# A graph layer on one core: key sums that begin with the rows left in SBUF, weights loaded between key blocks, rows split one at a time, edge lists loaded further apart

## The chip, the cores and the metric

The kernel runs on one core of a Trainium2 chip. TensorE (PE) multiplies matrices into PSUM; VectorE (DVE), ScalarE (ACT) and GpSimd (POOL) work on SBUF (POOL not on PSUM); SyncE (SP) here only issues DMAs. Each engine works through its own queue in order and waits on semaphores. The metric is the time of one execution in microseconds (us), lower is better; the runs of the kernel before lie within 0.12 us of each other.

## What is computed

One layer of a graph network with attention and a mixture of experts, on 12,500 nodes of 256 features with 200,000 edges of 8 types, sorted by destination:

```python
xn = _layernorm(x, axis=-1)
x = x + _L0_gnn_ref(xn, ...) + _L0_mix_ref(xn[None], ...)[0]
x = x + _L0_ffn_ref(_layernorm(x, axis=-1)[None], ...)[0]
```

The graph part multiplies each edge's source row by its weight, averages over the edges with the same type and destination, multiplies by that type's matrix and adds `x @ root + bias`. The mix part is linear attention: `q` and `k` go through `elu + 1`, `kv` and `k_sum` are sums over all nodes of `k` times `v` and of `k`, and each node's output is `q @ kv / (q @ k_sum)` through `wo`. The last part is a router over six experts of three layers, of which the best two are combined.

## The kernel before

Rows are worked on in *tiles* of 128 nodes (`NT`; 98 of them, `TILES_N`) and *row blocks* of four tiles (`SUB`; 25, `SUPER`, the last with two tiles). Products are made exact by splitting each factor into a high and a low part, three matmuls for one.

**First stage** (about 16 to 618 us). Per tile `u`, TensorE multiplies the normalised rows by all eight type matrices: four PSUM results of 512 columns, 24 matmuls, in three banks `yb` in turn (L769). ScalarE copies them into `yst` (L350; two buffers, `u % 2`), and SP stores `yst` to `y_tab` in HBM (L283). The copy into a buffer waits for the store of the tile two before (`y_out`). Per row block, SP also stores the transposed rows, high and low (`xhl`, two buffers), to `xt_tab`, stores `xs` to `x_tab` and loads the next `xs`. SP issues everything from one list, in which `edge_loads(u)` stands ahead of tile `u`'s store: four edge lists (`dst`, `etype`, `src`, `ew`; 125 rows of 1600 numbers each) at tiles 0 to 3, a copy of `dst` to `dpad` at tiles 5 and 6, padding of `etab` at tile 8. VectorE works on the lists in `edges(u)`, between the steps of the row blocks: at tile 5 it waits for all four lists (L641, then L642), from tile 5 on it uses `dst`, from tile 6 on `etype` and `src`, from tile 75 on `ew`. A barrier ends the stage.

**Key stage** (about 623 to 880 us). Twelve *portions* `p`; in the first nine (`KEYED`) the 98 tiles' keys and values are made, 11 tiles to a portion, 10 in the last (`keys_of`). Per tile `v`:

- TensorE: `key_product(v)`, six matmuls of the rows in `xk` with `wk` and `wv` (L1647), into one of three banks; then `key_sum_of(v - 2)`, four matmuls that add the tile into the sum (L1810);
- VectorE: `key_value(v)` adds the bias into `zv` (L1556), then `key_features(v - 1)` finishes `kf_c` (L1561);
- ScalarE: `key_parts(v)`, `ek_c` and `kf_c` (L1251, L1252).

`xk` has two halves of one row block each; SP loads block `d` from `xt_tab` (`load_xk`, L1080) when the products of block `d - 2` are done. Before its loads SP issues the edge tables `tab`, `wq` and `g_root` (into `xn_c`, whose split by ScalarE and VectorE comes ahead of VectorE's first `key_value`), and `xc`; then, between blocks 1 and 2, the first two experts' layers (`load_w`, into `stage`) and the router's. The third layer follows block 10.

Beside the keys, the first row block's edges are gathered (POOL, L1135, from `y_tab` into `ring`) and summed by TensorE, one portion of five or six edge tiles after each portion of keys (`aggregate(0, p - 1)`). Portions below 4 (`PLAIN`) are multiplied unsplit (L1704); from 4 on, ScalarE makes `row_hi` (`high`, L1192), VectorE `row_lo` (`low_rows`, L1379), and TensorE multiplies both (L1710). In key portions 5 to 8, ScalarE does the rows of portion `p - 1` in one go after the third tile, VectorE after the fifth. After portions 2, 5 and 9 (`WEIGHTS_AT`) ScalarE and VectorE split one layer of expert weights. `root(-1, FIRST)`, 24 matmuls, stands after portion 0.

**Last stage** (to the end): per row block, the attention's output, the experts, and the gathers and sums of the next row block.

SBUF names that share memory are allocated one over the other (`with ExitStack() as px`): `xk` lies over the third layer's high part, `zv` over later buffers.

Of the kernel before, what the change touches and what calls it, by code (L numbers as in the profile page):

```python
# [5 lines left out]
F32 = mybir.dt.float32  # L6
# [8 lines left out]
P = 128  # L15
KC = C // P
# [39 lines left out]
def gps_layer(nc, x, src, dst, etype, ew, g_w, g_root, g_b, wq, bq, wk, bk, wv, bv, wo, bo,  # L56
# [21 lines left out]
    with whole:  # L78
# [25 lines left out]
        eq = sbuf(whole, "eq", [P, KC, NS])  # L104

        pa = ExitStack()
        with pa:
# [12 lines left out]
            xhl = sbuf(pa, "xhl", [P, 2, 2, KC, NS], F32R)  # L120
# [66 lines left out]
            wkv_in, wr_in, small_in, bkv_in, rows_in_e, lin_in = (  # L187
                sem(n) for n in ("wkv_in", "wr_in", "small_in", "bkv_in", "rows_in_e", "lin_in"))
# [25 lines left out]
            def _(sp):  # L214
# [208 lines left out]
            def _(dve):  # L423
# [197 lines left out]
                def edges(u):  # L621
# [18 lines left out]
                    if u == 5:  # L640
                        dve.wait_ge(lin_in, 64)  # L641
# [3 lines left out]
                    if u == 6:  # L645
                        dve.tensor_copy(lin_tf, lin_t[0:ROWS, :])
# [188 lines left out]
        with pc:  # L835
# [53 lines left out]
            row_lo = sbuf(pc, "row_lo", [P, SLOTS, PT, C], F32R)  # L889
            xlo = sbuf(pc, "xlo", [P, C], F32R)  # L890
            with ExitStack() as px:
# [12 lines left out]
            xsel = sbuf(pc, "xsel", [P, NT], F32R)  # L904
# [123 lines left out]

            def keys_of(p):
# [17 lines left out]
            def _(sp):  # L1047
# [36 lines left out]
                load_xk(0)  # L1084
# [4 lines left out]
                load_xk(1)  # L1089
                load_table(1)  # L1090
                load_w(0, e_w1, 0)
# [791 lines left out]
```

## Time and profile before

| what | value |
|---|---|
| median of 3 runs | 3027.47 us (3027.4 to 3027.52) |
| the profiled execution's own time | 3028.82 us |
| its span, first to last instruction | 3027.3 us |
| mean granted TensorE clock | 0.988 of full speed |
| busy: PE, DVE, ACT, POOL | 97%, 72%, 58%, 55% |

A row of busy time gives the stretch and its length, then busy us and count of PE, of PE's weight loads (PEld), DVE, ACT and POOL, then three numbers: granted clock, busy share of the 16 DMA engines, GB/s moved. A row in order of time gives start, length, engine, line, operation, out<-in and, in brackets, the idle time before it with what ended it. SPq is SP's queue. A DMA row ends with KB each and us from issue to landing, where that is known.

### The profile page before, as it was taken

How to read it: one execution, taken by the hardware profiler on the slowest of the kernel's cores; microseconds unless marked ns; L12 is line 12 of the kernel's file. 1: busy time of each engine (PE TensorE's matmuls, PEld its weight loads, DVE VectorE, ACT ScalarE, POOL GpSimd, SP SyncE). 2: the span in 40 equal slices, each digit the busy share in tenths (PEclk: the TensorE clock that was granted, in tenths of full speed). 3: DMA queues.
4: the chain of work that ended last, by engine and by line, in shares of the span. 5: the costliest groups of instructions: out<-in, count | busy, mean ns of one | idle time of the engine just before them, and what ended most of it. 6: DMA issues, size and time to landing. Idle time of an engine off the chain costs nothing.

```text
span 3027.3 us, 47261 instructions
## 1 busy us (share of the span) xinstructions
PE 2934.1 (97%) x16707; PEld 2567.4 (85%) x16708; DVE 2189.2 (72%) x5317; ACT 1765.7 (58%) x3392; POOL 1659.3 (55%) x1700
## 2 busy tenths in 40 slices
PE   6999999969989999999999999999999999999998
PEld 5888878858778888888888888888888888888887
DVE  4479664125668787778888777788777778878775
ACT  3555555523446665666666566666666566666555
POOL 1000000042257777777777777777777777777740
PEclk9999999989999999999999999999999999999999
DMA  7677677875443444444444444443444444344420
GB/s 258 249 267 272 261 276 269 292 250 174 146 140 107 129 131 132 133 127 129 118 121 133 133 134 129 131 122 118 134 131 131 134 126 129 116 128 131 131 74 11
DMA packets 182224, 473.45 MB, mean 156 GB/s; under 512 B 46934, under 2 KB 105260, under 8 KB 159747
## 3 DMA queue, kind: packets, MB, share of 16 engines
q0 software_dynamic: 80544, 221.54, 25.4%
q1 hardware_dynamic: 99248, 247.02, 22.6%
q8 instruction: 133, 2.18, 0.3%
q10 hardware_dynamic: 2196, 1.86, 0.2%
q14 instruction: 103, 0.84, 0.1%
HBM read 312.80 MB, written 158.29 MB: 156 GB/s over the span
## 4 chain that ended last, share of the span: by engine, by line
PE 68%; DVE 6%; ACT 2%; DVEq 1%; issue 1%; DMA 1%; SPq 0%; ACTq 0%
PE bank L1647 45%; PE acc L1704 8%; PE acc L1710 8%; PE acc L1647 2%; DVE sel L1362 2%; PE bank L1674 1%; PE bank L1810 1%; DVE x L1457 1%; PE bank L1683 1%; PE bank L1693 1%; DVE stats_c L1461 1%; PE bank L1760 1%; DVEq L1459 1%; DVE h_lo L1487 1%; ACT h_hi L1205 1%
## 5 line engine op out<-in xcount | busy, mean ns | idle before, releaser
L1135 POOL DMA_INDIRECT ring<-y_tab,tab x1666 | 1642.6, 986 | 653.4 <-issue 497.5
L1205 ACT ACTIVATE h_hi<-bank,bias_t 128x512 fp32r<-128x512 f32 (+1 forms) x600 | 407.7, 679 | 315.6 <-PE bank L1647 280.1
L1487 DVE TENSOR_TENSOR h_lo<-bank,h_hi 128x512 fp32r<-128x512 f32 (+1 forms) x600 | 382.1, 675 | 228.1 <-ACT bank L1206 226.2
L769 PE MATMUL yb<-wr_hi,xhl 128*128 128x512 f32 x1568 | 509.4, 402 | 14.5 <-ACT yst L350 12.5
L1192 ACT ACTIVATE row_hi<-ring,tab 128x256 fp32r<-128x256 f32 x1091 | 449.6, 497 | 14.4 <-PE acc L1710 13.5
L1379 DVE SCALAR_TENSOR_TENSOR row_lo<-ring,tab,row_hi 128x256 fp32r<-128x256 f32 x1091 | 447.8, 478 | 7.8 <-ACT row_hi L1192 7.8
L350 ACT ACTIVATE yst<-yb 128x512 f32<-128x512 f32 x392 | 229.8, 596 | 273.6 <-PE yb L769 245.5
L1206 ACT ACTIVATE bank<-bank,bias_t 128x512 f32<-128x512 f32 (+1 forms) x600 | 386.3, 644 | 0.0
L769 PEld LDWEIGHTS yb<-wr_hi,xhl 128*128 128x128 f32 x1568 | 298.6, 190 | 88.8 <-ACT yst L350 15.2
L1647 PE MATMUL bank<-ew_hi,h_hi 128*128 128x256 f32 x1176 | 342.7, 291 | 1.5 <-DVE h_lo L1487 1.4
L1647 PE MATMUL bank<-ew_lo,h_hi 128*128 128x256 f32 x1176 | 329.1, 280 | 0.0
L1647 PE MATMUL bank<-ew_hi,h_lo 128*128 128x256 f32 x1176 | 328.9, 280 | 0.0
L769 PE MATMUL yb<-wr_lo,xhl 128*128 128x512 f32 x784 | 312.9, 399 | 0.0
L1710 PE MATMUL acc<-row_hi,hot_r 128*128 128x256 f32 x1091 | 270.5, 286 | 8.5 <-DVE row_lo L1379 8.5
L1710 PE MATMUL acc<-row_lo,hot_r 128*128 128x256 f32 x1091 | 268.0, 284 | 0.0
L1704 PE MATMUL acc<-ring,sel 128*128 128x256 f32 x1150 | 264.5, 379 | 0.0
L1647 PE MATMUL bank<-h_hi,ew_hi 128*128 128x512 f32 (+1 forms) x600 | 237.0, 395 | 2.0 <-DVE h_lo L1487 2.0
L1704 PEld LDWEIGHTS acc<-ring,sel 128*128 128x128 f32 x1150 | 214.4, 190 | 28.3
L1529 DVE SCALAR_TENSOR_TENSOR y<-bank,gate,y 128x256 f32<-128x256 f32 x490 | 211.6, 477 | 36.9 <-PE bank L1647 30.9
L1647 PE MATMUL bank<-h_hi,ew_lo 128*128 128x512 f32 (+1 forms) x600 | 234.2, 390 | 0.0
L1647 PE MATMUL bank<-h_lo,ew_hi 128*128 128x512 f32 (+1 forms) x600 | 234.2, 390 | 0.0
L1647 PE MATMUL bank<-ft_hi,ew_hi 128*128 128x512 f32 (+1 forms) x600 | 233.0, 388 | 0.0
(265 smaller groups left out, 5514.7 us busy)
## 6 DMA issues: line engine op xcount, KB each, us to landing
y_tab<-yst SPq DMA_DIRECT2D x97, 1024.0 KB, 4.1
ring<-y_tab,tab POOLq DMA_INDIRECT x1666, 2.8
xt_tab<-xhl SPq DMA_DIRECT2D x25, 1024.0 KB, 4.6
xk<-xt_tab SPq DMA_DIRECT2D x25, 1024.0 KB, 4.9
xc<-xt_tab SPq DMA_DIRECT2D x25, 1024.0 KB, 5.4
x<-x_tab SPq DMA_DIRECT2D x49, 256.0 KB, 3.2
xs<-in_x SPq DMA_DIRECT2D x24, 512.0 KB, 6.0
x_tab<-xs SPq DMA_DIRECT2D x24, 512.0 KB, 5.0
```

Of the source, the lines that this page charges most:

```text
L350: act.activation(yst[:, h, 2 * b:2 * b + 2, :], yb[(YB * u + b) % 3][:, :].rearrange("p (r n) -> p r n", r=2), ACT.Copy).then_inc(y_ev, 1)
L769: last = pe.matmul(out_ap, a, b, start=(i == 0), stop=(i == len(parts) - 1))
L1135: pool.indirect_dma_start(out=out_ap, out_offset=None, in_=y_tab[:, :], in_offset=bass.IndirectOffsetOnAxis(ap=idx_ap, axis=0)).then_inc(s ...
L1192: last = act.activation(row_hi[:, p % BUFS, q, :], ring[:, p % SLOTS, q, :], ACT.Copy, scale=tab[:, n % 2, t, k, 2:3])
L1205: act.activation(dest[:, m, 0:W], b[:, 0:W], ACT.Relu, bias=bias)
L1206: act.activation(b[:, 0:W], b[:, 0:W], ACT.Relu, bias=bias).then_inc(h_set, 1)
L1379: last = dve.scalar_tensor_tensor(out=row_lo[:, p % SLOTS, q, :], in0=ring[:, p % SLOTS, q, :], scalar=tab[:, n % 2, t, k, 2:3], in1=row_h ...
L1487: gone(dve.tensor_tensor(lo_[:, m, 0:W], bank[plan[kind, (e, m)][0]][:, 0:W], hi[:, m, 0:W].bitcast(F32), ALU.subtract))
L1529: last = dve.scalar_tensor_tensor(out=y[:, t, :], in0=b[:, (t % 2) * C:(t % 2 + 1) * C], scalar=gate[:, t, e:e + 1], in1=(y if e else x1)[ ...
L1647: last = pe.matmul(out_ap, a, b, start=(begin and i == 0), stop=(not more and i == len(parts) - 1), skip_group_check=more)
L1704: last = pe.matmul(sums(t), sel[:, p % BUFS, q, :], ring[:, p % SLOTS, q, :], start=False, stop=False, skip_group_check=True)
L1710: last = pe.matmul(sums(t), hot_r[:, p % BUFS, q, :], half, start=False, stop=False, skip_group_check=True)
```

## The change

The two `xhl` buffers, which hold the last two row blocks (23 and 24) at the end of the first stage, now live on into the key stage and are its `xk`; the key sums begin with these six tiles (`key_order`), and only blocks 0 to 22 are loaded, each when the half it goes into is done. The first layer's weights and the router's load after block 2, the second layer's after block 6. `high` and `low_rows` take a range of rows: counting a portion's tiles from 0, ScalarE does two rows after each of tiles 1 to 3, VectorE one after each tile from 5 on and the rest after the last. The edge lists load at tiles 0, 2, 4 and 8, each with a semaphore of its own, `dpad` at 11 and 12. `qf` and the third layer's high part move so that `xhl` can lie over them; `ek_c` has two buffers instead of three and lies elsewhere.

```diff
         eq = sbuf(whole, "eq", [P, KC, NS])
+        with ExitStack() as px:
+            xhl = sbuf(px, "xhl", [P, 2, 2, KC, NS], F32R)
+        w3_hi = sbuf(whole, "ew2_hi", [P, EXPERTS, KC, C], F32R)
+        qf = sbuf(whole, "qf", [P, KC, NS])
...
-            xhl = sbuf(pa, "xhl", [P, 2, 2, KC, NS], F32R)
...
                 def edge_loads(u):
-                    if u < 4:
-                        a, into = ((dst, lin_d), (etype, lin_t), (src, lin_s), (ew, lin_w))[u]
-                        sp.dma_start(into[0:ROWS, :], by_row(a)).then_inc(lin_in, 16)
+                    if u in (0, 2, 4, 8):
+                        i = (0, 2, 4, 8).index(u)
+                        a, into = ((dst, lin_d), (etype, lin_t), (src, lin_s), (ew, lin_w))[i]
+                        sp.dma_start(into[0:ROWS, :], by_row(a)).then_inc(lin_in[i], 16)
                     whole_tiles = E // P
-                    if u == 5:
+                    if u == 11:
                         sp.dma_start(dpad[0:whole_tiles, :].rearrange("(a t) k -> a (t k)", a=22),
                                      dst[0:whole_tiles * P].rearrange("(a k) -> a k", a=22)).then_inc(dpad_out, 16)
-                    if u == 6:
+                    if u == 12:
...
                     if u == 5:
-                        dve.wait_ge(lin_in, 64)
+                        dve.wait_ge(lin_in[0], 16)
...
                     if u == 6:
+                        dve.wait_ge(lin_in[1], 16)
+                        dve.wait_ge(lin_in[2], 16)
...
+                    if u == 75:
+                        dve.wait_ge(lin_in[3], 16)
...
-                ek = sbuf(px, "ek_c", [P, KEY_BUFS, C])
...
-            qf = sbuf(pc, "qf", [P, KC, NS])
...
-            with ExitStack() as px:
-                xk = sbuf(px, "xk", [P, 2, 2, KC, NS], F32R)
-            w_hi.append(sbuf(pc, "ew2_hi", [P, EXPERTS, KC, C], F32R))
+            w_hi.append(w3_hi)
+            xk = xhl
...
+            with ExitStack() as px:
+                ek = sbuf(px, "ek_c", [P, 2, C])
...
+            KEPT = SUPER - 2
+            key_order = list(range(SUB * KEPT, TILES_N)) + list(range(SUB * KEPT))
+
+            def key_place(d):
+
+                return d % 2 if d >= KEPT else (d + SUPER) % 2
...
                 def load_xk(d):
-                    if d >= 2:
-                        sp.wait_ge(key_proj, SUB * (d - 1))
-                    sp.dma_start(xk[:, d % 2, :, :, :].bitcast(F32).rearrange("p h k n -> p (h k n)"),
+                    sp.wait_ge(key_proj, SUB if d == 0 else SUB * d + LAST_T)
+                    sp.dma_start(xk[:, key_place(d), :, :, :].bitcast(F32).rearrange("p h k n -> p (h k n)"),
                                  xt_tab[d:d + 1, :, :].rearrange("a p n -> (a p) n")).then_inc(xk_in[d % 2], 16)
 
                 sp.sem_inc(y_stored, 16)
-                load_xk(0)
                 load_table(0)
                 for i, w in enumerate((wq, g_root)):
                     sp.dma_start(stage_q[:, i, :, :], w.rearrange("(k p) n -> p k n", p=P)).then_inc(wqr_in, 16)
                 load_xc(0)
-                load_xk(1)
                 load_table(1)
-                load_w(0, e_w1, 0)
-                sp.dma_start(stage_r[:, :, :], r_w1.rearrange("(k p) n -> p k n", p=P)).then_inc(w_in[0], 16)
-                load_w(1, e_w2, 1)
-                for d in range(2, SUPER):
+                for d in range(KEPT):
                     load_xk(d)
+                    if d == 2:
+                        load_w(0, e_w1, 0)
+                        sp.dma_start(stage_r[:, :, :], r_w1.rearrange("(k p) n -> p k n", p=P)).then_inc(w_in[0], 16)
+                    if d == 6:
...
 
-                def high(n, p):
+                def high(n, p, some=range(PT)):
                     if p >= parts(n):
                         return
-                    act.wait_ge(tab_in[n % 2], 16 * SUB * (n // 2 + 1))
-                    act.wait_ge(rows_in[p % SLOTS], 16 * gathers(n, p))
-                    tables_free(act, n, p)
-                    for q, (t, k) in enumerate(tiles_of_portion(p)):
+                    size = len(tiles_of_portion(p))
+                    if some[0] == 0:
+                        act.wait_ge(tab_in[n % 2], 16 * SUB * (n // 2 + 1))
+                        act.wait_ge(rows_in[p % SLOTS], 16 * gathers(n, p))
+                        tables_free(act, n, p)
+                    for q in range(some[0], min(some[-1] + 1, size)):
+                        t, k = tiles_of_portion(p)[q]
                         last = act.activation(row_hi[:, p % BUFS, q, :], ring[:, p % SLOTS, q, :],
                                               ACT.Copy, scale=tab[:, n % 2, t, k, 2:3])
-                    last.then_inc(hi_ready, 1)
+                    if some[-1] >= size - 1:
...
                     if p < KEYED:
                         for j, v in enumerate(keys_of(p)):
                             key_parts(v)
-                            if p > PLAIN and j == 2:
-                                high(0, p - 1)
+                            if p > PLAIN and 1 <= j <= PT // 2:
+                                high(0, p - 1, range(2 * j - 2, 2 * j))
...
 
-                def low_rows(n, p):
+                def low_rows(n, p, some=range(PT)):
                     if p >= parts(n):
                         return
-                    dve.wait_ge(hi_ready, split_before(n, p) + 1)
-                    for q, (t, k) in enumerate(tiles_of_portion(p)):
+                    size = len(tiles_of_portion(p))
+                    if some[0] == 0:
+                        dve.wait_ge(hi_ready, split_before(n, p) + 1)
+                    for q in range(some[0], min(some[-1] + 1, size)):
+                        t, k = tiles_of_portion(p)[q]
                         last = dve.scalar_tensor_tensor(out=row_lo[:, p % SLOTS, q, :], in0=ring[:, p % SLOTS, q, :],
                                                         scalar=tab[:, n % 2, t, k, 2:3],
                                                         in1=row_hi[:, p % BUFS, q, :].bitcast(F32),
                                                         op0=ALU.mult, op1=ALU.subtract)
-                    last.then_inc(lo_ready, 1)
+                    if some[0] < size <= some[-1] + 1:
+                        last.then_inc(lo_ready, 1)
...
-                            if p > PLAIN and j == 4:
-                                low_rows(0, p - 1)
+                            if p > PLAIN and j >= 5:
+                                low_rows(0, p - 1, range(j - 5, j - 4) if j < len(keys_of(p)) - 1 else range(j - 5, PT))
...
                 def key_product(v):
                     if v >= KEY_BUFS:
                         pe.wait_ge(key_z, v - KEY_BUFS + 1)
-                    d, nodes = v // SUB, slice(v % SUB * NT, (v % SUB + 1) * NT)
-                    in_parts(bank[KEY_BANKS[v % KEY_BUFS]][:, :], lambda k: xk[:, d % 2, 0, k, nodes], lambda k: xk[:, d % 2, 1, k, nodes],
+                    u = key_order[v]
+                    d, nodes = key_place(u // SUB), slice(u % SUB * NT, (u % SUB + 1) * NT)
+                    in_parts(bank[KEY_BANKS[v % KEY_BUFS]][:, :], lambda k: xk[:, d, 0, k, nodes], lambda k: xk[:, d, 1, k, nodes],
                              lambda k: wkv_hi[:, k, :], lambda k: wkv_lo[:, k, :]).then_inc(key_proj, 1)
...
-                    n = NT if v < TILES_N - 1 else LAST_ROWS
+                    n = NT if key_order[v] < TILES_N - 1 else LAST_ROWS
...
                     for v in keys_of(p):
-                        if v % SUB == 0:
-                            pe.wait_ge(xk_in[v // SUB % 2], 16 * (v // SUB // 2 + 1))
+                        u = key_order[v]
+                        if u % SUB == 0 and u < SUB * KEPT:
+                            pe.wait_ge(xk_in[u // SUB % 2], 16 * (u // SUB // 2 + 1))
```

## Rows read from the trace of the kernel before

**Rows 1.** Busy time by stretch (start:end, length, then each engine's busy us):
```profile
16.00:76.00 60.00, 49.39 (x185) 38.31 (x186) 26.82 (x44) 24.16 (x44) 3.25 (x12) 0.89 0.71 259
...
76.00:618.00 542.00, 539.73 (x2433) 436.35 (x2431) 306.06 (x490) 282.36 (x519) 7.58 (x6) 1.00 0.72 269
...
618.00:720.00 102.00, 78.40 (x386) 65.93 (x386) 42.61 (x90) 29.93 (x72) 41.29 (x44) 0.87 0.64 216
...
730.00:740.00 10.00, 10.00 (x57) 8.62 (x57) 5.93 (x12) 3.72 (x11) 0.00 (x0) 1.00 0.82 292
...
668.00:670.00 2.00, 2.00 (x19) 2.00 (x18) 0.33 (x1) 0.72 (x2) 1.39 (x3) 1.00 0.35 98
```

**Rows 2.** Waits from 0 to 130 us (total, times, longest):
```profile
ACT yst L350 <- DMA y_tab<-yst: 18.3, 3, 6.7
```

**Rows 3.** DMA issues in narrow windows (count, KB each, us to landing):
```profile
y_tab<-yst SPq DMA_DIRECT2D x1, 1024.0 KB, 17.0
...
lin_w<-in_edge_weight SPq DMA_DIRECT2D x1, 781.2 KB
```

**Rows 4.** Busy time in stretches of 2 us, columns as in Rows 1:
```profile
54.00:56.00 2.00, 1.36 (x3) 1.16 (x4) 0.34 (x2) 1.74 (x4) 0.00 (x0) 0.55 0.32 133
...
56.00:58.00 2.00, 2.00 (x7) 1.54 (x6) 0.00 (x0) 0.40 (x1) 0.00 (x0) 0.60 0.31 131
```

**Rows 5.** SP's queue in order of time, first 130 us:
```profile
36.88 0.62 SPq L283 DMA_DIRECT2D y_tab<-yst  x1
...
76.05 0.33 SPq L283 DMA_DIRECT2D y_tab<-yst  x1
...
99.33 0.32 SPq L283 DMA_DIRECT2D y_tab<-yst  x1
```

**Rows 6.** SP's queue in order of time, 620 to 690 us:
```profile
623.34 0.33 SPq L1080 DMA_DIRECT2D xk<-xt_tab  x1
625.09 3.71 SPq L1073 DMA_DIRECT2D tab<-etab  x4
...
630.35 0.43 SPq L1080 DMA_DIRECT2D xk<-xt_tab  x1
...
635.62 3.06 SPq L1065 DMA_DIRECT2D stage<-in_L_ffn_expert_w  x2
...
644.66 42.52 SPq L1080 DMA_DIRECT2D xk<-xt_tab  x5
```

**Rows 7.** TensorE in order of time, 636 to 662 us (in brackets: idle before):
```profile
639.93 0.71 PE L1810 MATMUL bank<-zv,kf_c 128*128 128x129 f32 x4 [3.39 <-DVE kf_c L1561]
...
659.18 0.79 PE L1647 MATMUL bank<-wkv_hi,xk 128*128 128x512 f32 x1 [7.76 <-DMA xk<-xt_tab]
```

**Rows 8.** Chain that ended last, 590 to 910 us:
```profile
642.56 0.86 PE bank L1810 x4
...
667.71 2.87 PE acc L1647 x24
...
683.17 0.45 PE bank L1810 x4
683.61 1.39 PE bank L1647 x6
```

**Rows 9.** Loads of xk alone, issues at 671.99 and 630.35:
```profile
xk<-xt_tab SPq DMA_DIRECT2D x1, 1024.0 KB, 5.1
...
xk<-xt_tab SPq DMA_DIRECT2D x1, 1024.0 KB, 10.9
```

**Rows 10.** Waits from 720 to 884 us:
```profile
PE bank L1810 <- DVE kf_c L1561: 10.5, 8, 3.4
```

**Rows 11.** VectorE and ScalarE in order of time, 769 to 782 us:
```profile
775.34 0.69 DVE L1556 TENSOR_TENSOR zv<-bank,kw_sb 128x512 f32<-128x512 f32 x1 [0.81 <-PE bank L1647]
...
776.51 2.46 DVE L1379 SCALAR_TENSOR_TENSOR row_lo<-ring,tab,row_hi 128x256 fp32r<-128x256 f32 x6
...
773.03 2.49 ACT L1192 ACTIVATE row_hi<-ring,tab 128x256 fp32r<-128x256 f32 x6
```

More of the change, by code:

```diff
@@ L186, in gps_layer @@
             wkv_hi_set, wkv_split = (sem(n) for n in ("wkv_hi_set", "wkv_split"))
-            wkv_in, wr_in, small_in, bkv_in, rows_in_e, lin_in = (
-                sem(n) for n in ("wkv_in", "wr_in", "small_in", "bkv_in", "rows_in_e", "lin_in"))
+            wkv_in, wr_in, small_in, bkv_in, rows_in_e = (
+                sem(n) for n in ("wkv_in", "wr_in", "small_in", "bkv_in", "rows_in_e"))
+            lin_in = [sem(f"lin_in{i}") for i in range(4)]
             pads_set, ident_set, consts_set, misc_full, misc_free = (
@@ L889, in gps_layer @@
             row_lo = sbuf(pc, "row_lo", [P, SLOTS, PT, C], F32R)
+            with ExitStack() as px:
+                ek = sbuf(px, "ek_c", [P, 2, C])
             xlo = sbuf(pc, "xlo", [P, C], F32R)
+            xsel = sbuf(pc, "xsel", [P, NT], F32R)
+            spare = sbuf(pc, "spare", [P, NT])
             with ExitStack() as px:
@@ L903, in gps_layer @@
             xtab_i = xtab[:, :].bitcast(I32)
-            xsel = sbuf(pc, "xsel", [P, NT], F32R)
             xrel = sbuf(pc, "xrel", [P, 1])
@@ L1088, in _ @@
                 load_xc(0)
-                load_xk(1)
                 load_table(1)
-                load_w(0, e_w1, 0)
-                sp.dma_start(stage_r[:, :, :], r_w1.rearrange("(k p) n -> p k n", p=P)).then_inc(w_in[0], 16)
-                load_w(1, e_w2, 1)
-                for d in range(2, SUPER):
+                for d in range(KEPT):
                     load_xk(d)
+                    if d == 2:
+                        load_w(0, e_w1, 0)
+                        sp.dma_start(stage_r[:, :, :], r_w1.rearrange("(k p) n -> p k n", p=P)).then_inc(w_in[0], 16)
+                    if d == 6:
+                        load_w(1, e_w2, 1)
                     if d == 10:
@@ L1183, in queries @@
                         act.activation(b[:, 0:NS], b[:, 0:NS], ACT.Relu, bias=bias_t[:, BQ + m:BQ + m + 1]).then_inc(q_set, 1)
-                def high(n, p):
+                def high(n, p, some=range(PT)):
                     if p >= parts(n):
                         return
-                    act.wait_ge(tab_in[n % 2], 16 * SUB * (n // 2 + 1))
-                    act.wait_ge(rows_in[p % SLOTS], 16 * gathers(n, p))
-                    tables_free(act, n, p)
-                    for q, (t, k) in enumerate(tiles_of_portion(p)):
+                    size = len(tiles_of_portion(p))
[5 more added lines that the diff above has]
+                        t, k = tiles_of_portion(p)[q]
                         last = act.activation(row_hi[:, p % BUFS, q, :], ring[:, p % SLOTS, q, :],
                                               ACT.Copy, scale=tab[:, n % 2, t, k, 2:3])
-                    last.then_inc(hi_ready, 1)
+                    if some[-1] >= size - 1:
+                        last.then_inc(hi_ready, 1)
                 def iteration(i, plan):
@@ L1250, in key_parts @@
                     z = zv[:, v % KEY_BUFS, 0:KC, 0:P]
-                    act.activation(ek[:, v % KEY_BUFS, :].rearrange("p (k n) -> p k n", k=KC), z, ACT.Exp)
+                    act.activation(ek[:, v % 2, :].rearrange("p (k n) -> p k n", k=KC), z, ACT.Exp)
                     act.activation(kf[:, v % 2, :].rearrange("p (k n) -> p k n", k=KC), z, ACT.Relu).then_inc(key_e, 1)
@@ L1560, in key_features @@
                     dve.wait_ge(key_e, v + 1)
-                    dve.scalar_tensor_tensor(out=kf[:, v % 2, :], in0=ek[:, v % KEY_BUFS, :], scalar=1.0, in1=kf[:, v % 2, :],
+                    dve.scalar_tensor_tensor(out=kf[:, v % 2, :], in0=ek[:, v % 2, :], scalar=1.0, in1=kf[:, v % 2, :],
                                              op0=ALU.min, op1=ALU.add).then_inc(key_f, 1)
```

## Prediction

> **What bounds the kernel now.** I read the busy time by stretch first: it says where TensorE, the engine of the whole kernel, is not busy. In the first stage (76 to 618 us) it is busy 539.7 of 542 us; what is lost lies in 16 to 76 us (10.6 us idle, granted clock 0.89) and in 618 to 720 us (23.6 us idle, clock 0.87) [rows 1]. The change touches both stretches, and the rest of the key stage besides. So each stretch needs its own question: which wait ends last there.
>
> In 16 to 76 us the waits say it: ScalarE, which copies PSUM to `yst`, waited three times, 18.3 us, for an earlier `y_tab` store out of the same buffer [rows 2]. Store 2 took 17.0 us to land [rows 3]. While ScalarE waits, only 0.32 and 0.31 of the 16 DMA engines work, at 133 and 131 GB/s [rows 4]: that is 5 of 16 (0.3125). The stage's other DMAs have 128 partitions, the edge lists 125 rows; so I read it as five engines carrying the lists, with every store's last five shares queued behind them. SP's queue gives the price: stores 2 to 6 lie 39.17 us apart, stores 6 to 10, with no list left, 23.28 [rows 5]. The lists cost 15.9 us.
>
> In 618 to 720 us TensorE has three holes: it starts only with its first `xk`, asked for at 623.34 [rows 6], waits 3.39 us for VectorE (639.93), and 7.76 us for its third `xk` (659.18) [rows 7]. SP's queue shows why the third is late: four weight loads of 768 KB and the router's 128 KB were issued from 635.62 on, and `xk` block 2 only at 644.66 [rows 6].
>
> **Part 1, edge lists spaced.** Bytes and instructions stay the same. One of five engines moves 132/5 = 26.4 GB/s [rows 4]; a list of 781.2 KB [rows 3] then holds the five for 6.0 us, a 1 MB transfer split over 16 holds each for 2.5, a half MB for 1.25. Four tiles (23.3 us) carry four stores, a transposed row block and two half MB, 15.0 us per engine; 8.3 us are spare, or 2.1 per tile. A list needs three tiles of spare time and gets two, then two, then four: the queue still grows, but half as much.
>
> I walk the five engines' queue. First before, as a test: free at an estimated 29.8 after list 0, then store 0, half MB, list 1, store 1, half MB, list 2, store 2: 29.8 + 3 x 2.5 + 2 x 1.25 + 2 x 6.0 = 51.8; it landed at 36.88 + 17.0 = 53.9 [rows 3, 5]. The walk is 2 us early, so I add 2. After the change one list fewer lies ahead of store 2: 47.8, 10.9 us after its issue. Then the transposed block and store 3 (5.0), the next list (6.0) and store 4 (2.5): 61.3, 11.2 us after an issue at about 50.1 (36.88 + 2 x 5.82 + 1.6). How late may a store be? The next tile (5.8) and three PSUM banks (3 x 1.4) pass before TensorE halts, less 0.7 for the copy: 9.3. The halts are 1.6 and 1.9, together 3.5; the fourth list, four tiles later, meets a drained queue. After a halt of 3 us the clock granted was 0.55 and 0.60 over 4 us [rows 4], which loses 1.7; I count 2.0 for both halts. Gain: 15.9 - 5.5 = 10.4. Bounds: no halt at all, 15.9; both stores 2.5 us later than walked, 5.
>
> `dpad` (781 KB, DRAM to DRAM) moves from tile 5 to 11; its reader waits in tile 27, some 90 us on, so I cost it at nothing; without that cover it would be one halt of 3 us. The list waits of VectorE are split; the second stands at tile 6 behind list 2 (walked to 58.8), and behind it queue VectorE's split of the next row block, which TensorE needs two tiles later, about 10 us: hidden. The wait for `lin_w` in tile 75 costs nothing: the list has then been in for some 350 us.
>
> **Part 2, key sums start with rows in SBUF.** Removed: two of 25 `xk` loads, and the wait of the first product. TensorE may start some 5 us earlier, but its fourth product waits for VectorE's `zv`, which comes behind its work on `wq` and `g_root`. Those loads move up by the removed issue, at most 625.09 - 623.34 = 1.75 us, at least 0 [rows 6]; I take 1.0. So the first key sum starts at 638.9, not 639.93 [rows 7]; product 3, which ended at 642.56 [rows 8], ends at 641.5. That asks for block 0 into the freed half. A load issued alone while gathers still ran took 5.1 us [rows 9]: it lands at 646.6. Two more tiles (1.84 each: 0.45 + 1.39 [rows 8]) and about 1.5 of half clock end at 646.7, so it just fits. Products 6 to 10 take 5 x 1.84, and `root` starts at 656.0 instead of 667.71 [rows 8]: 11.7. I take 11.5, for a little wait.
>
> The weights then follow block 2. It is asked for when product 9 ends, at about 653.6; behind it in the queue stand 1.70 MB of weights and, from 663.8, block 3. From 641.25 (630.35 + 10.9) to 659.15 SP's queue moved 4.33 MB beside the gathers [rows 6, 9]: 242 GB/s. Block 2, weights and block 3 are 3.80 MB, 15.7 us and some 1.5 to land: 670.8. Product 18 needs block 3 at 656.0 + 2.87 + 7 x 1.84 = 671.7. It fits by 0.9 us. The second weights follow block 6, when the gathers have slowed; the third load shows such a meeting (730 to 740 us, DMA at 0.82, TensorE busy 10.0 of 10 [rows 1]). Bounds for the part: block 0 late by 3 us with a half-clock stretch behind it, and block 3 late by 1.5: 6; a prologue 1.75 earlier: 12.5.
>
> A rule speaks against this. The gathers run in the other queue, at 98 GB/s when alone [rows 1]. The Trainium skill, "DMA: Bandwidth & Descriptors", section "Queues, rings and completion order", says that each DMA engine goes round the queues that have work, a packet from each. By that, the gathers could take half of each engine, block 0 would land some 2.5 us later, and the part would give 9 instead of 11.5. The 5.1 us of the load at 672, gathers beside it, do not bear this out; it is case (f) below.
>
> **Part 3, rows one by one.** The same 23 splits. The eight waits of TensorE for `kf_c` in 720 to 884 us sum to 10.5 [rows 10]; two, 2.9 and 3.4, are the weight splits and stay, about 4.1 are the six-row bursts of 2.46 (VectorE) and 2.49 us (ScalarE) [rows 11] and the stage's end. In pieces they fit: a row costs VectorE 0.41, and it sits idle 0.81 per tile [rows 11]; two rows cost ScalarE 0.83 beside its 0.72 per tile of 1.84. That gains 3.3. Against it: in portions 5 and 7 the last row comes after the portion's last tile, and the aggregate waits for it: `zv` 0.65, `kf_c` 0.42 and the row 0.41 end 1.5 after the last product, where 0.3 was the case: 1.2. In portion 5 the weight split's wait swallows it; portion 7 pays it. At the end two rows come ahead of the last `kf_c`: 0.4. Net 1.5; bounds -1 and 3.3. The smaller `ek` costs nothing: a third copy was never in use, for key sum v-2 must be done before `ek` v is written.
>
> **Sum.** 10.4 + 11.5 + 1.5 = 23.4. The profiled execution took 3028.82 around a span of 3027.3; the median of the runs is 3027.47, 1.35 less. I take the sum from the median: 3004.1 us.
>
> **Rivals.** (a) The halts of the first stage persist, since the lists still ride on five engines: gain 5 there, 18 in all, 3009.5. For it: the walk missed by 2 us, and both late stores lie under 2 us past the limit. (b) Loads late in the key start, block 0 and then block 3 behind the weights: 6 instead of 11.5, 3009.6. The margin of block 0 is 0.1 us, that of block 3 is 0.9. (c) Nothing moves, because the losses reappear as other waits (VectorE's prologue in the key stage, five engines in the first): 3027. Against it: TensorE is idle or at half clock there, and behind these stretches it is busy all the time. (d) Slower: each `xk` load is asked for only when its half is free, four tiles or 7.34 us ahead. If the mean landing, 5.1 here, rose past 7.34 + 23.4/23 = 8.36 us in all 23 loads, the gain would be gone; at 9.5 us, 3030. Against it: the lead is the same as in the kernel before, where loads behind no weights cause no wait. (e) Better: no halts and no late row, under 2997. (f) The gathers take half of each engine while both queues have work: 16 x 26.4 = 422 GB/s [rows 4] halved makes 5.0 us of a load's 2.5, so block 0 lands at 649.1 and the part gives 9: 3006.6. For it: block 0 does fall among the gathers; against it: at 98 GB/s they use a quarter of 422.
>
> **Chances.** Forecast 0.62 (own range 2999 to 3009), (a) 0.15, (b) 0.08, (c) 0.04, (d) 0.02, (e) 0.04, (f) 0.05. From 2996 to 3014 leaves out (c), (d), part of (e), and (a) where (b) joins it. Under 3021.4 is faster by over 0.2%, about what a measurement here can tell: 0.94; within 0.2% 0.04; slower 0.02.
>
> **What would show it.** Right: stores 2 to 6 about 29 us apart; two short halts in the first 80 us; no wait for `xk` over 1 us after the key stage's start; `root` near 656; no 1 us holes in portions 5 to 8 but a wait for `row_lo` before portion 7's aggregate. Wrong: halts of 3 us as before, a product at 647 or 671 that waits for its load, or a new wait for `kf_c` in each tile that carries rows.

## The result, and the profile after

The changed kernel takes 2992.3 us (median of 4 runs, 2990.83 to 2996.88) against 3027.43 (4 runs) beside it: a ratio of 0.989, 95% interval 0.9876 to 0.9904. The gain is 35.1 us where 23.4 were predicted, and the time lies under the range. The profiled execution is the slowest of the four (2996.88 us, span 2995.4), so its parts sum to 31.9 us.

The kernel after, busy time by stretch, columns as in [rows 1]:

```profile
16.00:76.00 60.00, 53.95 (x226) 43.16 (x227) 33.33 (x59) 28.93 (x53) 3.31 (x12) 0.97 0.74 281
76.00:600.00 524.00, 518.69 (x2390) 427.98 (x2388) 299.38 (x476) 276.90 (x508) 7.60 (x6) 1.00 0.74 276
600.00:720.00 120.00, 101.94 (x512) 86.20 (x512) 58.93 (x124) 38.70 (x96) 49.76 (x50) 0.90 0.65 213
```

The first and third rows are what the prediction was about. The second is the surprise. TensorE was busy 539.7 of 542 us there before [rows 1] and is busy 518.7 of 524 now: hardly less full, yet the stage ends sooner than store 6 explains. SP's queue of the kernel after, in order of time (it answers to [rows 5]), and the last store before:

```profile
36.81 0.33 SPq L288 DMA_DIRECT2D y_tab<-yst  x1
...
65.35 0.32 SPq L288 DMA_DIRECT2D y_tab<-yst  x1
...
89.98 0.32 SPq L288 DMA_DIRECT2D y_tab<-yst  x1
...
600.80 0.33 SPq L288 DMA_DIRECT2D y_tab<-yst  x1
```
```profile
618.54 0.33 SPq L283 DMA_DIRECT2D y_tab<-yst  x1
```

Stores 2 to 6 lie 28.54 us apart, and store 6 goes out 10.7 us earlier, as forecast. But the last store is 17.7 us earlier: between store 10, 9.35 us earlier, and the last another 8.4 came in, over 87 tiles. TensorE in order of time in a stretch of 2 us without a halt, first before, then after:

```profile
399.72 0.63 PE L769 MATMUL yb<-wr_hi,xhl 128*128 128x512 f32 x2
400.18 0.39 PE L769 MATMUL yb<-wr_lo,xhl 128*128 128x512 f32 x1
400.42 0.63 PE L769 MATMUL yb<-wr_hi,xhl 128*128 128x512 f32 x2
...
401.12 0.63 PE L769 MATMUL yb<-wr_hi,xhl 128*128 128x512 f32 x2
```

```profile
399.87 0.61 PE L778 MATMUL yb<-wr_hi,xhl 128*128 128x512 f32 x2
400.32 0.39 PE L778 MATMUL yb<-wr_lo,xhl 128*128 128x512 f32 x1
400.55 0.61 PE L778 MATMUL yb<-wr_hi,xhl 128*128 128x512 f32 x2
...
401.23 0.61 PE L778 MATMUL yb<-wr_hi,xhl 128*128 128x512 f32 x2
```

Three products take 0.70 us before and 0.68 after: a start every 233 and every 227 ns, of the same instructions, at a granted clock of 1.00 in both. Busy time can't show that, since a slower product is as busy as a quick one.

The key stage of the kernel after, TensorE in order of time (it answers to [rows 7]; in brackets the idle time before), two pieces of the chain ([rows 8]; start, length, what), and last TensorE in the kernel before:

```profile
599.75 0.39 PE L778 MATMUL yb<-wr_hi,xhl 128*128 128x512 f32 x1
607.35 0.79 PE L1670 MATMUL bank<-wkv_hi,xhl 128*128 128x512 f32 x1 [7.21 <-DVEq L1329]
...
621.69 1.23 PE L1834 MATMUL bank<-zv,kf_c 128*128 128x129 f32 x4 [7.18 <-DVE kf_c L1584]
...
631.13 0.50 PE L1670 MATMUL bank<-wkv_hi,xhl 128*128 128x512 f32 x1 [0.75 <-DMA xhl<-xt_tab]
...
695.60 0.80 PE L1834 MATMUL bank<-zv,kf_c 128*128 128x129 f32 x2 [2.92 <-DVE kf_c L1584]
...
848.27 0.58 PE L1733 MATMUL acc<-row_hi,hot_r 128*128 128x256 f32 x1 [6.41 <-DVE row_lo L1401]
```

```profile
625.51 5.57 DMA xhl<-xt_tab
...
640.55 2.87 PE acc L1670 x24
```

```profile
617.48 0.40 PE L769 MATMUL yb<-wr_hi,xhl 128*128 128x512 f32 x1
630.15 0.77 PE L1647 MATMUL bank<-wkv_hi,xk 128*128 128x512 f32 x1 [12.27 <-DMA xk<-xt_tab]
...
722.63 0.71 PE L1810 MATMUL bank<-zv,kf_c 128*128 128x129 f32 x4 [2.92 <-DVE kf_c L1561]
...
882.75 0.58 PE L1710 MATMUL acc<-row_hi,hot_r 128*128 128x256 f32 x1 [6.41 <-DVE row_lo L1379]
```

TensorE starts earlier after the first stage (7.21 us instead of 12.27), waits more for the first key sum (7.18 instead of 3.39), and reaches `root` some 40 us after the stage's end instead of 50. No load of `xk` is waited for longer than 0.75 us.

For all runs I read three lengths from such rows. S is the issue of the last `y_tab` store. K runs from the end of the stage's last product to the product behind the 2.9 us wait (here 600.14 to 695.60: 95.46). R runs from there to aggregate(0, 9) (to 848.27: 152.67). Behind that the program does the same work: an undisturbed iteration takes 87.60 us in both. S, K and R are each read from one profiled execution.

### The profile page after: what moved, and what is told of

Same layout as the page of the kernel before. It is cut to its first block, busy times and chain, and to the rows that moved or that the text cites. A ratio compares the mean times of both kernels' runs of the same rounds, so it can differ in the third digit from the quotient of the medians.

```text
span 2995.4 us, 47258 instructions
## 1 busy us (share of the span) xinstructions
PE 2914.0 (97%) x16707; PEld 2561.0 (85%) x16708; DVE 2190.0 (73%) x5317; ACT 1762.9 (59%) x3392; POOL 1674.2 (56%) x1700
## 4 chain that ended last, share of the span: by engine, by line
PE 63%; POOL 6%; DVE 5%; issue 3%; ACT 1%; DVEq 1%; DMA 0%; SPq 0%; ACTq 0%; POOLq 0%
PE bank L1670 41%; PE acc L1727 7%; PE acc L1733 7%; POOL ring L1150 6%; PE acc L1670 2%; DVE sel L1381 2%; PE bank L1834 1%; PE bank L1697 1%; DVE x L1480 1%; PE bank L1706 1%; PE bank L1716 1%; DVE h_lo L1510 1%; DVE stats_c L1484 1%; PE bank L1783 1%; DVEq L1482 1%
## 5 line engine op out<-in xcount | busy, mean ns | idle before, releaser
L778 PE MATMUL yb<-wr_hi,xhl 128*128 128x512 f32 x1568 | 498.2, 394 | 13.1 <-ACT yst L355 11.1
L1210 ACT ACTIVATE row_hi<-ring,tab 128x256 fp32r<-128x256 f32 x1091 | 451.7, 498 | 33.3 <-issue 17.7
L778 PE MATMUL yb<-wr_lo,xhl 128*128 128x512 f32 x784 | 306.9, 391 | 0.0
L1733 PE MATMUL acc<-row_hi,hot_r 128*128 128x256 f32 x1091 | 270.1, 286 | 10.7 <-DVE row_lo L1401 10.7
```

What stands on the lines that cost most here:

```text
L778: last = pe.matmul(out_ap, a, b, start=(i == 0), stop=(i == len(parts) - 1))
L1210: last = act.activation(row_hi[:, p % BUFS, q, :], ring[:, p % SLOTS, q, :], ACT.Copy, scale=tab[:, n % 2, t, k, 2:3])
L1733: last = pe.matmul(sums(t), hot_r[:, p % BUFS, q, :], half, start=False, stop=False, skip_group_check=True)
```

## The experiments

| kernel | median, us | ratio to before (95%) | S | K | R |
|---|---|---|---|---|---|
| before | 3027.47 | | 618.54 | 104.75 | 160.12 |
| changed | 2992.30 | 0.9890 (0.9876 to 0.9904) | 600.80 | 95.46 | 152.67 |
| e11_changed_again | 2995.06 | 0.9888 (0.9873 to 0.9903) | 599.60 | 95.63 | 152.68 |
| e1_moved_32 | 3011.58 | 0.9945 (0.9928 to 0.9961) | 605.18 | 105.34 | 158.68 |
| e8_both_at_0 | 3015.99 | 0.9955 (0.9938 to 0.9971) | 607.74 | 104.73 | 158.45 |
| e3_back_96 | 3001.57 | 0.9912 (0.9896 to 0.9929) | 607.74 | 95.57 | 152.23 |
| e2_lists_only | 3015.48 | 0.9958 (0.9941 to 0.9974) | 608.54 | 105.22 | 155.77 |
| e4_lists_back | 3002.59 | 0.9916 (0.9900 to 0.9933) | 609.73 | 95.47 | 151.62 |
| e5_rows_one_go | 2999.47 | 0.9901 (0.9884 to 0.9917) | 600.12 | 95.21 | 158.52 |
| e13_rows_only | 3023.92 | 0.9990 (0.9981 to 0.9998) | 618.18 | 105.08 | 152.98 |
| e7_keys_by_number | 3005.20 | 0.9919 (0.9900 to 0.9939) | 599.08 | 105.34 | 156.03 |
| e6_weights_first | 3007.24 | 0.9934 (0.9921 to 0.9947) | 599.60 | 106.56 | 155.54 |
| e14_weights_between_only | 2995.22 | 0.9895 (0.9878 to 0.9913) | 599.34 | 94.27 | 152.76 |
| e10_h_moved_64 | 2996.88 | 0.9893 (0.9877 to 0.9910) | 599.11 | 95.19 | 155.65 |
| e12_rows_112_13 | 2987.59 | 0.9862 (0.9845 to 0.9880) | 589.89 | 96.04 | 151.64 |
| e15_rows_112_13_alone | 2985.55 | 0.9863 (0.9846 to 0.9881) | 588.92 | 95.18 | 152.68 |

The first three runs of the kernel before lie within 0.12 us of each other, but those beside the experiments spread from 3022.3 to 3033.5, and most medians here are of four runs: a difference of 2 or 3 us between two of them says little.

**Where `xhl` lies.** By the addresses in the compiled programs `xhl`, the stationary operand of stage one, moved from 78720 to 30368 bytes (modulo 128: from 0 to 32); `wr_hi`, the moving one, is at 32 modulo 128 in both kernels. e1_moved_32 is the kernel before with 32 bytes ahead of `xhl`:

```diff
+            sbuf(pa, "gap0", [P, 8])
             xhl = sbuf(pa, "xhl", [P, 2, 2, KC, NS], F32R)
+            sbuf(pa, "gap1", [P, 24])
```

> The kernel before, with `xhl` alone moved up by 32 bytes in each partition (from 78720 to 78752; nothing that the matmuls of stage one read besides it moves). Theory 'place': the 512-column products of stage one start every 227 ns in the changed kernel against 234 ns before since the address of `xhl` modulo 128 went from 0 to 32 bytes. Then the stage's mean pace falls to 227 ns here too, stage one ends near 609 us instead of 617.9, and the whole takes about 3019 us. Rival 'region': what counts is that `xhl` lies at 30368 and no longer at 78720 among the tiles that DVE and ACT write; then 32 bytes change nothing, the pace stays 234 ns and the time 3027. Rival 'spacing': the pace has to do with the edge lists; then 3027 too.

e3_back_96 undoes it in the changed kernel:

```diff
+            sbuf(px, "gap0", [P, 24])
             xhl = sbuf(px, "xhl", [P, 2, 2, KC, NS], F32R)
...
         qf = sbuf(whole, "qf", [P, KC, NS])
+        sbuf(whole, "gap1", [P, 32])
```

> The changed kernel with `xhl` (which is `xk` too) moved up by 96 bytes, to an address that is a multiple of 128; all other tiles keep their address modulo 128. Theory 'place': the pace of stage one goes back to 234 ns, stage one ends near 608 us instead of 600, and the whole takes 7 to 9 us longer, about 3000 us. Rivals 'region' and 'spacing': no change, 2992 us.

e8_both_at_0 is the kernel before with the moving operand brought to the stationary one's place:

```diff
+            sbuf(pa, "gap0", [P, 24])
             wr_hi = sbuf(pa, "wr_hi", [P, KC, REL, C], F32R)
             wr_lo = sbuf(pa, "wr_lo", [P, KC, REL, C], F32R)
+            sbuf(pa, "gap1", [P, 8])
```

> The kernel before with `wr_hi` and `wr_lo`, the moving operands of stage one, moved up by 96 bytes to multiples of 128, and `xhl`, the stationary one, kept at a multiple of 128. If what counts is that both operands have the same address modulo 128 (theory 'same place'), the pace is 227 ns and the time about 3012 us. If what counts is where the stationary operand lies by itself (theory 'own place': a multiple of 128 is the slow place), the pace stays 234 ns and the time 3027.

TensorE's groups by shape from 320 to 430 us (the last number before the second bar is the mean ns of one), in this order: before, after, e1, e3, e8:

```profile
L769 PE MATMUL yb<-wr_hi,xhl 128*128 128x512 f32 x302 | 96.5, 397 | 0.0
```
```profile
L778 PE MATMUL yb<-wr_hi,xhl 128*128 128x512 f32 x307 | 96.3, 391 | 0.0
```
```profile
L771 PE MATMUL yb<-wr_hi,xhl 128*128 128x512 f32 x305 | 95.9, 392 | 0.3 <-ACT yst L352 0.3
```
```profile
L780 PE MATMUL yb<-wr_hi,xhl 128*128 128x512 f32 x300 | 96.0, 397 | 0.0
```
```profile
L771 PE MATMUL yb<-wr_hi,xhl 128*128 128x512 f32 x306 | 96.1, 392 | 0.3 <-ACT yst L352 0.3
```

The lists are the old ones in e1 and e8 and the spaced ones in e3, and the pace follows the addresses in all three: quick when both operands lie at the same address modulo 128 (32 and 32, or 0 and 0), slow when they do not. "Region", "spacing" and "own place" fall. These pairs agree or differ modulo 256 as well, so the modulus itself is not shown. The price is 13.4 us of S in e1 (its forecast had some 9), 10.8 in e8, and 6.9 to 8.1 in e3 against the two runs of the changed kernel. One reason why it is not the whole of 6 ns for each of 2352 products is that a quicker TensorE runs into the stores: behind store 10 it waits 4.9 us for `yst` in the changed kernel and 4.8 in e1, 2.1 before. Why it is smaller beside the spaced lists is not shown.

In the key stage the rule does not show, though its products are 512 columns wide too. A tile's six products and key sum recur every 1.83 us in the changed kernel, with `xhl` and `wkv_hi` both at 32, and every 1.84 in e3, with `xhl` at 0; six times 6 ns would have made 0.04 between them. First the changed kernel, then e3, the first product of a tile and of the next:

```profile
668.13 0.48 PE L1670 MATMUL bank<-wkv_hi,xhl 128*128 128x512 f32 x1
...
669.96 0.48 PE L1670 MATMUL bank<-wkv_hi,xhl 128*128 128x512 f32 x1
```
```profile
678.96 0.48 PE L1672 MATMUL bank<-wkv_hi,xhl 128*128 128x512 f32 x1
...
680.80 0.48 PE L1672 MATMUL bank<-wkv_hi,xhl 128*128 128x512 f32 x1
```

**Edge lists.** e2_lists_only is the kernel before with the diff's edits to `edge_loads` and its waits alone; e4_lists_back undoes them in the changed kernel.

> The kernel before with only the edge lists spaced (tiles 0, 2, 4, 8; the copies of dst after tiles 11 and 12). By the prediction's first term store 6 comes 10.4 us earlier and the whole takes 3017 us. If spacing the lists also set the faster pace of the rest of stage one (rival 'spacing'), stage one ends 17 to 18 us earlier and the whole takes about 3010 us.

> The changed kernel with the edge lists loaded at tiles 0 to 3 as before, all else as changed. By theory 'place' and the prediction's first term the loss is that of the spacing alone: store 6 about 10.7 us later, the pace still 227 ns, the whole about 3003 us. By rival 'spacing' the pace goes back to 234 ns and the whole takes about 3010 us.

S is 10.0 us earlier in e2 and 8.9 to 10.1 later in e4, while a `wr_hi` product takes 397 ns in e2 and 392 in e4: the first term by itself, with no part in the pace. Whether five engines are the reason was tried by cutting each list in two, and the later store of `seg_tab`, also of 125 rows, likewise:

```diff
-                        sp.dma_start(into[0:ROWS, :], by_row(a)).then_inc(lin_in[i], 16)
+                        sp.dma_start(into[0:112, :], by_row(a)[0:112, :]).then_inc(lin_in[i], 16)
+                        sp.dma_start(into[112:ROWS, :], by_row(a)[112:ROWS, :]).then_inc(lin_in[i], 16)
```

> The changed kernel with three things more. Each edge list is loaded by two transfers, of 112 and of 13 rows, instead of one of 125; the store of `seg_tab` is cut likewise; and `h1_hi` to `x1` are moved up by 64 bytes as in the run before. The prediction's first term says that a list of 125 rows goes to 5 of the 16 engines, and that the stores of `y_tab` behind it wait for those five. If that is right, 112 rows go to all 16, the two halts of 1.9 and 2.8 us between stores 2 and 6 go away, and stores 2 to 6 are 23 to 24 us apart instead of 28.5; the halt of 2.8 us at tile 67 to 69 shrinks likewise. With 0.25 us from each of 24 iterations the whole takes 12 us less than the changed kernel. If the halts come from the bytes alone (rival), stores 2 to 6 stay 28 us apart, and the gain is the 6 us of the iterations.

> The changed kernel with the lists and the store of seg_tab cut into 112 and 13 rows, and nothing moved: stage one ends near 590 us as with the tiles moved too, and each iteration takes 87.60 us. About 10 us less than the changed kernel in the profile, 2983 to 2985 us; with the tiles moved too it was 2987.6 since several iterations then lost a microsecond.

The kernel e15, first busy time from 16 to 76 us, then SP's queue in order of time:

```profile
16.00:76.00 60.00, 58.66 (x255) 47.98 (x256) 38.04 (x69) 32.39 (x59) 3.33 (x12) 1.00 0.89 319
```
```profile
37.42 0.34 SPq L290 DMA_DIRECT2D y_tab<-yst  x1
...
60.08 0.32 SPq L290 DMA_DIRECT2D y_tab<-yst  x1
```

In the same 60 us the 16 DMA engines are now busy 0.89 of the time instead of 0.74 and move 319 GB/s instead of 281, both halts of the changed kernel (1.89 and 2.82 us, at 46.6 and 59.9 us) are gone, stores 2 to 6 are 22.66 us apart, and behind store 10 the longest wait for `yst` is 0.7 us instead of 2.8. So the halts did not come from the bytes alone. S is 10.7 to 11.9 us earlier than in the changed kernel: 6.0 to 7.2 of that was gained by store 10, from the lists, and some 4.7 behind it, where the store of `seg_tab` was the other thing cut. The median is 6.8 and 9.5 us under the changed kernel's two. e12 has the same stage (stores 2 to 6 23.15 us apart, S 589.89) but is only 4.7 and 7.5 under, where 12 were forecast: with the tiles moved several iterations take about 1 us more. e15 is the best version of all: its four runs (2983.52 to 2986.6) lie wholly under the changed kernel's two sets. The Trainium skill, "DMA: Bandwidth & Descriptors", section "Why a DMA increments its semaphore by 16 and not by 1", says that a transfer uses the largest number of engines up to 16 that divides the outermost size of both its sides. By that rule 125 rows get 5 engines and 112 get 16; the 0.31 and 0.32 of [rows 4] and the row above agree.

**The key start.** e7_keys_by_number undoes the order and the place of the weights together; e6_weights_first undoes the place of the weights alone; e14_weights_between_only undoes the order alone. The lines of the order, in e7 and e14 (the loads of blocks 0 and 1 move back ahead with them):

```diff
-            key_order = list(range(SUB * KEPT, TILES_N)) + list(range(SUB * KEPT))
+            key_order = list(range(TILES_N))
...
-                return d % 2 if d >= KEPT else (d + SUPER) % 2
+                return d % 2
```

> The changed kernel with the key sums in the order of the numbers again: block 0 is loaded first, all 25 blocks are loaded, and the weights are loaded ahead of block 2. `xk` stays where the changed kernel has it. By the prediction's second term the loss is 11.5 us (bounds 6 to 12.5). By what the trace after shows (root begins 40.2 us after the end of stage one instead of 49.6) it is 9.4, about 3001.5 us.

> The changed kernel with the expert weights of the first two layers loaded ahead of all key blocks again, the key order as changed. The prediction put all of the second term on the key order and said that weights behind block 2 merely fit. If that is right, weights first make block 0 late: it lands behind 3.1 MB of weights, some 15 us later than now, and PE waits for it before the ninth product; the whole takes 5 to 15 us longer, 2997 to 3007 us. If the loads run side by side and block 0 needs them not to wait, there is no change.

> The changed kernel with the key sums in the order of the numbers (block 0 first, all 25 blocks loaded), but the expert weights between the blocks, as changed. It is the run with keys by number and only the weights moved back. With both undone the stretch from the end of stage one to the wait of 2.9 us in portion 3 was 105.3 us, with the weights alone undone 106.6, with neither 95.5. If the weights behind block 2 were what made block 2 late (it landed 14.5 us after its issue, PE waited 7.8), this run gives 97 to 98 us: the 7.5 to 8 us wait is gone, and only the later first product is left. If both are needed (theory 'together'), it stays near 105.

K decides: 95.5 us in the changed kernel, 105.3 with both undone, 106.6 with only the weights first, 94.3 with only the order undone. TensorE in order of time, with the weights first, and then the waits of TensorE from 598 to 700 us (total, times, longest) with the old order:

```profile
606.15 0.80 PE L1668 MATMUL bank<-wkv_hi,xhl 128*128 128x512 f32 x1 [7.21 <-DVEq L1327]
621.15 1.23 PE L1832 MATMUL bank<-zv,kf_c 128*128 128x129 f32 x4 [9.31 <-DVE kf_c L1582]
639.63 0.79 PE L1668 MATMUL bank<-wkv_hi,xhl 128*128 128x512 f32 x1 [9.99 <-DMA xhl<-xt_tab]
```
```profile
PE bank L1673 <- DMA xhl<-xt_tab: 11.6, 1, 11.6
PE bank L1837 <- DVE kf_c L1587: 7.5, 2, 4.6
```

With weights first, TensorE starts as early as in the changed kernel and then stands 9.99 us before block 0, which is queued behind the weights: the early start is given back whole. With the old order it starts 4.4 us later, but the wait of the first key sum shrinks from 7.18 to 4.60, and no later block is waited for. So the whole gain of the part belongs to the weights; the order adds none. In K it costs about 1.2 us where the weights have already moved; the whole times (2995.22 in e14, 2995.06 in e11) show no difference.

**Rows one by one.** e5_rows_one_go undoes it in the changed kernel, e13_rows_only makes it alone in the kernel before.

```diff
-                            if p > PLAIN and 1 <= j <= PT // 2:
-                                high(0, p - 1, range(2 * j - 2, 2 * j))
+                            if p > PLAIN and j == 2:
+                                high(0, p - 1)
...
-                            if p > PLAIN and j >= 5:
-                                low_rows(0, p - 1, range(j - 5, j - 4) if j < len(keys_of(p)) - 1 else range(j - 5, PT))
+                            if p > PLAIN and j == 4:
+                                low_rows(0, p - 1)
```

> The changed kernel with the first group's rows split in one go, as before. By the prediction's third term the loss is 1.5 us (bounds a gain of 1 and a loss of 3.3). By the reading of the trace after ('clock stays up': the product after portion 5 takes 1.63 us instead of 2.91, and those behind it stay at the full clock), the holes of 3 us and the half clock behind them come back and the loss is 4 to 6 us: about 2997 us against 2992.

> The kernel before with only the rows split one by one. The prediction's third term says 1.5 us. By the profiled executions so far, the stretch from the wait of 2.9 us in portion 3 to the start of aggregate(0, 9) is 152 to 156 us with the split one by one and 156 to 160 without, so the gain should be 4 to 5 us: 3022 to 3023 us.

The waits of TensorE in the stretch R, first of the kernel after (they answer to [rows 10]), then of e5:

```profile
PE acc L1733 <- DVE row_lo L1401: 10.7, 4, 6.4
PE bank L1834 <- DVE kf_c L1584: 6.1, 4, 2.9
```
```profile
PE bank L1834 <- DVE kf_c L1584: 10.6, 8, 3.5
PE acc L1733 <- DVE row_lo L1401: 8.6, 2, 6.4
```

The waits alone move by 2.4 us, and R by 5.85. Most of the rest is the clock. Busy time just behind the weight split's wait (a wait of 2.12 us in the changed kernel, 3.47 in e5, 2.13 in e7, 3.42 in e2) and behind a wait of 2.1 us for `row_lo`; first after, then e5, then e7 and e2 (first place only):

```profile
767.50:771.50 4.00, 3.97 (x22) 3.46 (x23) 2.71 (x6) 3.04 (x10) 2.94 (x3) 1.00 0.35 98
833.10:836.10 3.00, 2.94 (x18) 2.65 (x19) 3.00 (x8) 0.62 (x3) 2.39 (x3) 1.00 0.44 128
```
```profile
766.80:770.80 4.00, 3.96 (x12) 3.38 (x13) 1.78 (x4) 1.13 (x4) 2.93 (x3) 0.50 0.35 98
836.50:839.50 3.00, 2.97 (x13) 2.78 (x14) 3.00 (x7) 0.51 (x2) 2.39 (x3) 0.58 0.44 128
```
```profile
775.80:779.80 4.00, 3.94 (x15) 3.39 (x15) 2.03 (x5) 1.95 (x6) 2.93 (x3) 0.57 0.77 309
```
```profile
786.40:790.40 4.00, 3.96 (x22) 3.43 (x23) 2.69 (x5) 2.21 (x8) 2.93 (x3) 1.00 0.51 174
```

TensorE got through 22 matmuls in 4 us at the upper level (1.00) where e5 got through 12 at the lower (0.50). After a wait of the same length e7 fell to 0.57 all the same, and e2, which splits the rows in one go, kept 1.00 behind 3.42 us: the shorter wait doesn't ensure the full clock, nor does the longer one rule it out. TensorE fell to half clock there in four of the five kernels without the edit and in three of the eleven with it (e6, e7, e10). Over these 16 R is 155.8 to 160.1 us (mean 158.3) without the edit and 151.6 to 156.0 (mean 153.3) with it: 5.0 us. The lowest without it is e2, which kept the clock, and the highest with it e7, which lost it; of kernels whose clock did the same there, those with the edit are about 3 us shorter. The whole times say less: 2.5 us in e13 (ratio 0.9990), and 4.4 us in e5 against the changed kernel on the same chip (2999.47 and 2995.06).

**The rule of places, tried elsewhere.** `h1_hi`, a moving operand of the experts' second layer, lies at 96 modulo 128, its stationary `ew1_hi` at 32. e10_h_moved_64 brings them together:

```diff
+            sbuf(pc, "gap0", [P, 16])
             with ExitStack() as ps:
                 stage = [sbuf(ps, f"stage{i}", [P, EXPERTS, KC, C]) for i in range(2)]
```

> The changed kernel with `h1_hi` to `x1`, the moving operands of the experts' second layer among them, moved up by 64 bytes: `h1_hi` goes from 96 to 32 bytes past a multiple of 128, where `ew1_hi`, the stationary operand, lies. The second layer's products start every 233 ns now, the first layer's (both operands at 32) every 227. Theory 'same place': they go to 227 too, 1800 products gain 6 ns each, and the whole takes 11 us less, about 2981 us. Theory 'own place' (the stationary operand's address alone): no change, 2992 us.

TensorE's groups by shape from 1000 to 2000 us, columns as above, first of the kernel after, then of e10:

```profile
L1670 PE MATMUL bank<-ew_hi,h_hi 128*128 128x256 f32 x552 | 161.0, 292 | 0.0
...
L1670 PE MATMUL bank<-h_lo,ew_hi 128*128 128x512 f32 x275 | 108.3, 394 | 0.0
```
```profile
L1671 PE MATMUL bank<-ew_hi,h_hi 128*128 128x256 f32 x552 | 162.8, 295 | 0.0
...
L1671 PE MATMUL bank<-h_lo,ew_hi 128*128 128x512 f32 x276 | 107.6, 390 | 0.0
```

The 512-column products gain 4 ns of mean length (start to start 227 ns instead of 233), so the rule holds here too; the third layer's 256-column products, whose stationary operand is `h`, lose 3, though they too now have both operands at 32. An undisturbed iteration takes 87.35 us instead of 87.60, but several take about 1 us more, and the whole shows no gain where 11 us were forecast. So the rule is shown for the 512-column products of stage one and of the experts' second layer, and not for others. e11_changed_again, the changed kernel once more, gave the second measure used above:

> The changed kernel itself, once more, on the chip of the three runs that follow, as their measure. 2992 us; if the profiled execution of the changed kernel lost 3 us or more to the clock that others don't lose (2996.88 against a median of 2992.3), this one's spans are shorter.

## Why the prediction was wrong, point by point

**The step that failed** is in the first paragraph: "In the first stage (76 to 618 us) it is busy 539.7 of 542 us; what is lost lies in 16 to 76 us ... and in 618 to 720 us". It took busy for fast. The diff moves `xhl`, the stationary operand of all 2352 products of that stage, and the sum has no term for a tile that moves. The term is 6.9 to 8.1 us in the changed kernel, and it alone carries the time past the range: with it undone (e3) the kernel takes 3001.57 us.

**Part 1** was right: 10.4 predicted, 10.0 in e2 and 8.9 to 10.1 in e4; stores 2 to 6 about 29 us apart, measured 28.54; and e15 shows that the five engines are the reason. The two halts came where they were walked to, but took 4.7 us together instead of 3.5.

**Part 2** had the size nearly right (11.5; K says 9.3) and put it on the wrong half of the edit. As it foresaw, TensorE's early start mostly lengthened its wait for VectorE: the first key sum came 0.5 us earlier (21.55 instead of 22.05 us after the stage), where 1.0 was taken. Block 0 landed 5.57 us after its issue; 5.1 had been taken and rival (f) wanted some 2.5 more, so (f) fails, and a wait of 0.75 us was the only one for a load. What paid was block 2 no longer behind weights. The working names those weights as the reason for the third hole, but its sum has no term for them apart from the order, and so could not tell which half pays.

**Part 3** foresaw the two new waits for `row_lo` and the vanished 1 us holes. It mis-sized the term, 1.5 against 5.0 in R, chiefly by leaving out the half clock behind the 3.4 us wait, which fell less often with the shorter one. It had counted just that loss in part 1. The whole times (2.5 and 4.4 us) leave the size less sure than R does.

The sum as measured in the profiles: 10 for the lists, 7.5 for the place of `xhl`, 9.3 for the weights and 5 for the rows make 31.8; the profiled span fell by 31.9. That the two meet so closely is partly luck: in this pair R fell by 7.45, and the last stage took 2.5 longer in the profiled execution of the changed kernel, for a reason that stays open. The first set of runs gained 35.1 and the second 31.4 (3026.45 to 2995.06); why these differ stays open. So does how much of part 3 the clock gives back from run to run. Rival (d) of the prediction has a slip that nothing rests on: with 23 loads a mean landing of 9.5 us makes about 3054 us, not 3030.

## What to carry to other kernels

When an edit moves a tile that a matmul reads, give the move a term of its own, and compare start to start of the same product before and after; a full busy row hides it. Undo one half of a two-part edit at a time: here the order of the key sums, which the title names first, was worth nothing, and the moved weight loads all of that part. A transfer's row count is worth a look as well as its schedule: with the lists already spaced, cutting 125 rows into 112 and 13 took another 10.7 to 11.9 us off the stage (the store of `seg_tab` included). Cutting without spacing was not tried.

## What the hardware showed that I had not expected

In stage one and the experts' second layer a 512-column product with its operands at different addresses modulo 128 (32 or 64 bytes apart) started every 233 ns, and every 227 with both at the same one, at a granted clock of 1.00; the key stage's did not follow this. The Trainium skill, "TensorE: Matmul & The Clock Gate", section "Wait — 56ns, not 53.3ns?", gives 215.7 ns for 512 columns at the full clock and no second pace; the rows here show neither that figure nor one pace only, and the rows decide. A wait of 2.1 us was followed by the full clock in one execution and by 0.57 in another (e7), and one of 3.4 us by 0.50 in e5 and by 1.00 in e2.
